# A graph network block: block addresses computed ahead of the adds, and the attention sums' self-loops scaled group by group

## The chip, the cores and the metric

The kernel runs on one core of one Trainium2 chip. The metric is device time of one execution, in microseconds, as the median of several runs. An engine has a queue of its own (its sequencer), which waits for semaphores, loads registers, computes addresses and hands instructions to the engine. PE is TensorE, DVE VectorE, ACT ScalarE, POOL GpSimd, SP SyncE.

## The reference

A graph of 6250 nodes with 256 features and 106,250 edges (each node has an edge to itself, a self-loop, besides 100,000 drawn edges). In order: a normalisation; a graph convolution added to linear attention; a mixture of 8 experts; graph attention with 8 heads of 32 features, added to a second linear attention; and a mixture of 4 experts whose gates come from a second graph attention (131,072 edges, their ends drawn from 8192 numbers, 6250 of which are nodes).

```python
# graph convolution
agg = jax.ops.segment_sum(x[src], dst, num_segments=n)
# graph attention; a loop edge is added to every node
e = a_src[src] + a_dst[dst]
e = jnp.where(e > 0, e, NEG_SLOPE * e)
ex = jnp.exp(e - m[dst])
alpha = ex / (denom[dst] + 1e-16)
out = jax.ops.segment_sum(h[src] * alpha[:, :, None], dst, num_segments=N)
# router: the same attention with 4 heads of 4, then the two best of 4 experts
```

## The kernel before

Nodes are held in 49 blocks (the code calls them windows, W = 49) of 128, one node per partition. Edges are sorted by target block and cut into slots of 128 edges, four slots to a group (GROUP = 4). Four stages walk over groups: the prelude (33 groups, with keys and values of the first linear attention), stage 1 (187 groups, with the 8 experts), stage 2 (220 groups, with keys and values of the second linear attention) and stage 3 (268 groups, with the 4 experts). The order on every engine is written out by hand, and semaphores tie the engines together.

In each group POOL gathers the rows of the edges' source nodes with four indirect DMAs (L365, L1446, L2438, L3086), into a ring of 6, 5, 8 and 10 groups in the four stages. DVE makes a one-hot matrix from the edges' targets, PE multiplies it with the rows (L2468 in stage 2), and DVE adds the four products to the four blocks' sums (L471, L1786, L2659, L3293). Which block a slot belongs to is known only at run time. `windows` loads the four block numbers of a group into registers with one instruction (a TENSOR_LOAD in the trace), and `bass.ds(ws[u], 1)` selects a block; its address is worked out by an instruction of the engine's queue (a FUSED_REGOPS in the trace) in front of the instruction that first uses it. Each add waits for the one before it (s_acc). In stage 2 each also waits for its own product (s_sum); elsewhere one wait per group is enough, since the four products share one count.

In the attention stages (2 and 3) a group takes more steps. PE multiplies the transposed one-hot with the blocks' target scores (`scores`: L2456, L3104), which needs the block numbers too. DVE reduces and adds (`exponents`: L2632, L2636, L2642), ACT takes exponentials, and DVE scales the gathered rows (`message`: L2650). In stage 2 the DVE queue works in this order: load of block numbers, exponents of q + 2, one-hot of q + 5 (L2621), the four adds of q, message of q + 2. For the first 150 groups, one group in three then has the variance of the keys (L2663, L2668, L2669), and the next one the scaling of the values (L2673, L2678); groups 157 to 205 have one add of 128x256 (L2701). POOL's gather of group q + 8 waits for PE's sums of group q.

The self-loops need no gather: R.gat holds each node's own row, [128, 49, 264], 256 features and 8 weights. After the weights' exponential (s_e0) DVE multiplies the features of all 49 blocks by them in one instruction (L2732), ahead of one_hot(4) and of the loop over groups:

```python
v.wait_ge(self.s_e0, 1)
a4 = R.gat[:, :, 0:self.FEAT].rearrange("p t (h c) -> p t h c", h=GH)
st.then(v.tensor_tensor(a4, a4, R.gat[:, :, self.FEAT:GROW].unsqueeze(3).to_broadcast([P, W, GH, GC]), ALU.mult))
one_hot(4)
```

gperm lists the blocks in the order in which groups come to them: a group q has no target outside the first 4q + 4 of the list.

## Time and profile before

| What | us |
|---|---|
| Median of 3 runs | 4643.39 (4642.45 to 4644.51) |
| Span of the profiled execution | 4628.2 |
| What lies around the span, by the median | 15.2 |
| Prelude, first to last add | 229.2 to 400.5 |
| Stage 1, first to last add | 480.0 to 1650.1 |
| Stage 2, first gather, first add, last add's start | 1957.1, 1987.9, 3134.8 |
| Stage 2, end of the last gather of group 2, of group 3 | 1973.0, 1990.9 |
| Stage 3, first gather, last gather, last add's start | 3228.3, 4582.5, 4610.4 |

The profile gives the span of its execution, not its whole time; the last line of the upper part is the median less the span. PE is busy for 82% of the span, DVE for 69%, POOL for 61%, ACT for 49%. These shares are averages over stages that have different limits, so what follows is read stage by stage. "Idle before" a group of instructions is the time in which its engine stood still just ahead of them, and "<-" names what ended it; "issue" means that nothing in the trace was waited for, so that the queue itself was late.

### The profile page before, as it was taken

To read this page: it belongs to the slowest core of one execution; us is meant where nothing else is said; L and a number is where in the kernel's file an instruction comes from. 1 tells how busy PE (TensorE), PEld (TensorE's weight loads), DVE (VectorE), ACT (ScalarE), POOL (GpSimd) and SP (SyncE) were. 2 spreads that over 40 slices of the span, in tenths; PEclk is the share of its full clock that TensorE was granted. 3 is DMA by queue.
4 is the path that set the end of the run, shared out by engine and by line. 5 is a ranking of instruction groups with operands and counts; after the bars stand their busy time and mean duration, and the time that the engine had idled before them with its cause. 6 is when DMAs were issued, how large, how long until landed. Compare 5 with 4: busy or idle time off the path is not lost. (4 is left out here: it accounts for less than half of the span.)

```text
span 4628.2 us, 67760 instructions
## 1 busy us (share of the span) xinstructions
PE 3772.5 (82%) x17777; PEld 2396.7 (52%) x17779; DVE 3181.4 (69%) x10005; ACT 2264.5 (49%) x4090; POOL 2802.1 (61%) x2880
## 2 busy tenths in 40 slices
PE   6797989999989999678888888876187888887876
PEld 6654556666656566444444445445144444444444
DVE  7675566554645554688888888886567777777776
ACT  6342223323232332357767765444366666666665
POOL 0174676665655500177766777773777777777774
PEclk9998999999999999888889988995588889898887
DMA  3333111121211100545555545653322222222221
GB/s 98 77 90 106 39 40 41 32 43 31 43 29 38 26 8 2 160 122 141 141 133 132 132 127 156 163 141 95 56 35 44 40 40 39 39 40 40 39 39 26
DMA packets 291738, 331.33 MB, mean 72 GB/s; under 512 B 80182, under 2 KB 246062, under 8 KB 291366
## 3 DMA queue, kind: packets, MB, share of 16 engines
q0 software_dynamic: 105328, 175.77, 18.5%
q1 hardware_dynamic: 186038, 151.23, 11.8%
q8 instruction: 156, 2.56, 0.2%
q14 instruction: 216, 1.77, 0.1%
HBM read 289.56 MB, written 30.77 MB: 69 GB/s over the span
## 5 line engine op out<-in xcount | busy, mean ns | idle before, releaser
L3086 POOL DMA_INDIRECT st_rows<-tabr,router_rsrc x1072 | 1028.7, 960 | 329.7 <-issue 318.8
L2438 POOL DMA_INDIRECT all_XT<-tab,graph_gsrc x880 | 852.1, 968 | 310.3 <-issue 244.2
L1446 POOL DMA_INDIRECT st_rows<-tab,graph_gsrc x748 | 741.4, 991 | 465.3 <-PE st_pe L1469 262.2
L1699 ACT ACTIVATE st_h<-st_ph,st_shift,st_scale 128x448 f32<-128x448 f32 x448 | 324.0, 723 | 729.6 <-PE st_ph L1557 729.5
L2468 PE MATMUL st_po<-all_XT,st_hot 128*128 128x264 f32 x1760 | 572.5, 462 | 36.6 <-DVE gat_sum L2659 35.3
L2659 DVE TENSOR_TENSOR gat_sum<-gat_sum,st_po 128x264 f32 x880 | 376.0, 427 | 144.8 <-DVE gat_sum L2659 97.9
L3131 PE MATMUL st_px<-all_XT,st_w 128*128 128x512 f32 (+2 forms) x832 | 427.3, 664 | 18.5 <-ACT st_hid L3191 18.5
L2468 PEld LDWEIGHTS st_po<-all_XT,st_hot 128*128 128x128 f32 x1760 | 323.4, 213 | 198.6 <-DVE gat_sum L2659 120.2
L3143 PE MATMUL st_py<-st_w,st_hid 128*128 128x256 f32 x1568 | 424.9, 418 | 0.6 <-ACT st_hid L3191 0.6
L1786 DVE TENSOR_TENSOR gcn_acc<-gcn_acc,st_pe 128x65 f32 x748 | 166.2, 222 | 348.4 <-PE st_pe L1469 257.8
L3104 PE MATMUL st_pad<-st_adr,st_hott 128*128 x1072 | 123.2, 184 | 338.6 <-DVE st_zd L3257 323.6
L1570 PE MATMUL st_po<-all_XT,st_h 128*128 128x256 f32 x1568 | 373.5, 390 | 12.8 <-DVE all_X L1890 9.3
L1557 PE MATMUL st_ph<-st_h,all_XT 128*128 128x448 f32 x896 | 355.3, 547 | 3.3 <-ACT st_h L1699 3.3
L1557 PE MATMUL st_ph<-st_xt,all_XT 128*128 128x448 f32 x896 | 356.9, 552 | 0.0
L1570 PEld LDWEIGHTS st_po<-all_XT,st_h 128*128 128x128 f32 x1568 | 297.9, 195 | 67.5 <-issue 15.1
L3143 PEld LDWEIGHTS st_py<-st_w,st_hid 128*128 128x128 f32 x1568 | 308.0, 207 | 46.1 <-ACT st_hid L3191 1.0
L3104 PEld LDWEIGHTS st_pad<-st_adr,st_hott 128*128 128x128 bf16 x1072 | 87.5, 98 | 446.6 <-issue 425.0
L3293 DVE TENSOR_TENSOR router_racc<-router_racc,st_po 128x60 f32 x1072 | 229.8, 214 | 118.0 <-DVE router_racc L3293 3.2
L3180 ACT ACTIVATE st_rows<-st_d 128x16 f32<-128x16 f32 x268 | 57.9, 216 | 516.9 <-DVE st_d L3267 511.6
L3131 PEld LDWEIGHTS st_px<-all_XT,st_w 128*128 128x128 f32 x832 | 176.1, 223 | 192.0 <-issue 166.5
L1890 DVE SCALAR_TENSOR_TENSOR all_X<-st_po,st_gate,all_X 128x256 f32 x392 | 168.6, 478 | 144.9 <-PE st_po L1570 127.8
L2650 DVE TENSOR_TENSOR all_XT<-all_XT,st_wps 128x1024 f32<-128x1024 f32 x220 | 267.0, 1214 | 0.5 <-ACT all_XT L2575 0.5
(517 smaller groups left out, 7187.1 us busy)
## 6 DMA issues: line engine op xcount, KB each, us to landing
st_bc<-drowr SPq DMA_DIRECT2D x268, 128.0 KB
st_bc<-drow SPq DMA_DIRECT2D x220, 128.0 KB
st_rows<-tabr,router_rsrc POOLq DMA_INDIRECT x1072
all_XT<-tab,graph_gsrc POOLq DMA_INDIRECT x880
st_xtb<-xtd SPq DMA_DIRECT2D x98, 128.0 KB
st_rows<-tab,graph_gsrc POOLq DMA_INDIRECT x748
tab<-gat_sum SPq DMA_DIRECT2D x7, 924.0 KB
xtd<-all_XT SPq DMA_DIRECT2D x49, 128.0 KB, 1.7
```

The costliest lines, as they stand in the source:

```text
L1446: g.indirect_dma_start(self.rows[:, b, u, :], None, self.R.tab0, bass.IndirectOffsetOnAxis(self.R.gsrc[:, t:t + 1], 0)).then_inc(self.s_ro ...
L1557: mm = t.matmul(self.ph[:, m % 3, 0:HALF], (self.w1, self.w2)[l][:, e, i, fb * P:(fb + 1) * P], src[:, i, h * HALF:(h + 1) * HALF], start= ...
L1570: mm = t.matmul(self.po[:, q % 2, j - 2 * k, :], self.h2[:, i, j * P:(j + 1) * P], self.wo[:, e, i, :], start=(i == 0), stop=(i == C - 1))
L1699: a.activation((self.h1, self.h2)[l][:, fb, h * HALF:(h + 1) * HALF], self.ph[:, m % 3, 0:HALF], ACT.Relu, bias=self.shift[:, l, i:i + 1], ...
L2438: g.indirect_dma_start(self.rows[:, b, u, :], None, self.R.tab1, bass.IndirectOffsetOnAxis(self.R.gsrc[:, t:t + 1], 0)).then_inc(self.s_ro ...
L2468: t.matmul(self.po[:, m % self.BANKS, 0:GROW], self.hot[:, q % self.HOTF, u], self.rows[:, q % self.ROWS, u, :], start=True, stop=True).th ...
L2650: v.tensor_tensor(m, m, self.wps[:, :, :].unsqueeze(3).to_broadcast([P, GROUP, GH, GC]), ALU.mult)\
L2659: v.tensor_tensor(aw, aw, self.po[:, (GROUP * q + u) % self.BANKS, 0:GROW], ALU.add).then_inc(self.s_acc, 1)
L3086: g.indirect_dma_start(self.rows[:, b, u, :], None, self.R.tabr, bass.IndirectOffsetOnAxis(self.R.rsrc[:, t:t + 1], 0)).then_inc(self.s_ro ...
L3131: mm = t.matmul(self.px[:, i, 0:n * P], self.w1[:, e, c, fb * P:(fb + 1) * P], R.XT[:, c, r * P:(r + n) * P], start=(c == 0), stop=(c == C ...
L3143: t.matmul(self.py[:, m % 2, 0:D], self.hid[:, (E1 * u + e) % 2, fb, j * P:(j + 1) * P], self.w2[:, e, fb, :], start=(fb == 0), stop=False)
L3293: v.tensor_tensor(aw, aw, self.po[:, q % self.SUMB, u * n:(u + 1) * n], ALU.add).then_inc(self.s_acc, 1)
```

## The change

Four places are touched. `placed` has an engine work out addresses at once. In the prelude, stage 1, stage 2 and stage 3, DVE computes the four blocks' addresses right behind the load of the block numbers, at the group's head; in the prelude and stage 1 that is now ahead of the one-hot as well. PE does the same for `scores` in stages 2 and 3, ahead of its two waits. And in stage 2 the one multiply of the self-loops is gone: in the first 13 groups `own_edges` loads four entries of gperm and multiplies those four blocks, 49 blocks in all, and the adds of these groups wait for s_a0.

```diff
+def placed(engine, aps):
+    for ap in aps:
+        engine.lower_ap(ap)
+    return aps
+
+def columns_of(tile, ws):
+    return [tile[:, bass.ds(w, 1), :].rearrange("p a d -> p (a d)") for w in ws]
...
         def add_edges(q):
+            aws = placed(v, columns_of(acc, self.windows(ENG.DVE, q)))
             one_hot(q + self.HOTS - 1)
-            ws = self.windows(ENG.DVE, q)
             v.wait_ge(self.s_sum, q + 1)
-            for u in range(GROUP):
+            for u, aw in enumerate(aws):
                 if GROUP * q + u:
                     v.wait_ge(self.s_acc, GROUP * q + u)
-                aw = acc[:, bass.ds(ws[u], 1), :].rearrange("p a d -> p (a d)")
                 v.tensor_tensor(aw, aw, self.pe[...], ALU.add).then_inc(self.s_acc, 1)
...
         def scores(q):
-            ws = self.windows(ENG.PE, q)
+            near = placed(t, [self.adl[:, bass.ds(w, 1), :, :].rearrange("p a k h -> p (a k h)")
+                              for w in self.windows(ENG.PE, q)])
             t.wait_ge(self.s_tt, q + 1)
...
+        def own_edges(q):
+            lo, hi = GROUP * q, min(GROUP * q + GROUP, W)
+            if lo >= hi:
+                return
+            _, ws = self.nc.values_load_multi_w_load_instructions(
+                R.gperm[0:1, lo:hi], engines=(ENG.DVE,), min_val=0, max_val=W - 1, ...)
+            for w in ws:
+                a = R.gat[:, bass.ds(w, 1), 0:self.FEAT].rearrange("p a (h c) -> p (a h) c", h=GH)
+                x = R.gat[:, bass.ds(w, 1), self.FEAT:GROW].rearrange("p a h -> p (a h)")
+                v.tensor_tensor(a, a, x.unsqueeze(2).to_broadcast([P, GH, GC]), ALU.mult).then_inc(self.s_a0, 1)
+
+        def add(q, aws):
+            if GROUP * q < W:
+                v.wait_ge(self.s_a0, min(GROUP * q + GROUP, W))
...
         v.wait_ge(self.s_e0, 1)
-        a4 = R.gat[:, :, 0:self.FEAT].rearrange("p t (h c) -> p t h c", h=GH)
-        st.then(v.tensor_tensor(a4, a4, R.gat[:, :, self.FEAT:GROW].unsqueeze(3).to_broadcast([P, W, GH, GC]), ALU.mult))
         one_hot(4)
         for q in range(self.GROUPS):
-            ws = self.windows(ENG.DVE, q)
+            aws = placed(v, columns_of(R.gat, self.windows(ENG.DVE, q)))
+            own_edges(q)
             exponents(q + 2)
             one_hot(q + 5)
-            add(q, ws)
+            add(q, aws)
```

Stage 1's `add_edges` and stage 3's `scores`, `add` and loop get the same edit as the ones shown.

## Rows read from the trace of the kernel before

**Rows 1.** The page: its first line.

```profile
span 4628.2 us, 67760 instructions
```

**Rows 2.** Groups by line: count, busy us, mean ns; then idle before, by releaser.

```profile
L3086 POOL DMA_INDIRECT st_rows<-tabr,router_rsrc x1072 | 1028.7, 960 | 329.7 <-issue 318.8 <-DVE st_part L3284 7.6 <-POOLq L73 3.2
L2438 POOL DMA_INDIRECT all_XT<-tab,graph_gsrc x880 | 852.1, 968 | 310.3 <-issue 244.2 <-PE st_po L2468 65.8 <-POOL st_diag L1010 0.3
...
L2659 DVE TENSOR_TENSOR gat_sum<-gat_sum,st_po 128x264 f32 x880 | 376.0, 427 | 144.8 <-DVE gat_sum L2659 97.9 <-PE st_po L2468 46.8
```

**Rows 3.** Window: length; busy us of PE, PEld, DVE, ACT, POOL; clock, DMA share, GB/s.

```profile
2050.00:2800.00 750.00, 635.69 (x2378) 357.45 (x2376) 631.80 (x1472) 524.42 (x1008) 539.24 (x567) 0.90 0.53 136
```

**Rows 4.** Waits of POOL, 2100 to 2800 us: total us, times, longest.

```profile
POOL all_XT L2438 <- PE st_po L2468: 53.1, 49, 2.5
```

**Rows 5.** Timeline of DVE, one group of stage 2: start, duration, line.

```profile
2499.98 0.36 DVE L2632 TENSOR_REDUCE st_zd<-st_pad 128x64 f32<-128x192 f32 x1 [0.30 <-issue]
2500.38 0.22 DVE L2636 TENSOR_TENSOR st_z<-st_zd,all_XT 128x64 f32<-128x64 f32 x1
...
2501.71 0.43 DVE L2659 TENSOR_TENSOR gat_sum<-gat_sum,st_po 128x264 f32 x1 [0.21 <-DVE gat_sum L2659]
...
2503.34 1.21 DVE L2650 TENSOR_TENSOR all_XT<-all_XT,st_wps 128x1024 f32<-128x1024 f32 x1
...
2504.70 0.69 DVE L2678 TENSOR_TENSOR all_XT<-all_XT,st_rs 128x512 f32<-128x512 f32 x1
2505.31 0.35 DVE L2632 TENSOR_REDUCE st_zd<-st_pad 128x64 f32<-128x192 f32 x1
```

**Rows 6.** Timeline of DVE in stage 3: four adds, next group's first reduction.

```profile
3902.86 1.28 DVE L3293 TENSOR_TENSOR router_racc<-router_racc,st_po 128x60 f32 x4
...
3906.02 0.26 DVE L3257 TENSOR_REDUCE st_zd<-st_pad 128x32 f32<-128x96 f32 x1 [0.23 <-issue]
```

**Rows 7.** Line 3293: its adds, ns least, median, most.

```profile
L3293 DVE TENSOR_TENSOR router_racc<-router_racc,st_po x1072: 201/216/219, 3249.5 to 4610.4; 128x60 f32 x179
```

**Rows 8.** Line 3360: address instructions on DVE's queue (FUSED_REGOPS), and updates.

```profile
L3360 DVEq FUSED_REGOPS  x126: 57/57/57, 3384.1 to 4619.0; - x126
L3360 DVE SCALAR_TENSOR_TENSOR all_X<-all_XT,router_gate,all_X x110: 473/477/485, 3493.0 to 4621.7; 128x256 f32 x110
L3360 DVE SCALAR_TENSOR_TENSOR all_X<-st_py,router_gate,all_X x86: 473/483/486, 3384.2 to 4286.6; 128x256 f32 x86
```

**Rows 9.** Lines 2659 and 2382: address instructions, and loads of block numbers.

```profile
L2659 DVEq FUSED_REGOPS  x880: 57/57/57, 1987.5 to 3134.7; - x176
...
L2382 DVEq TENSOR_LOAD <-graph_gwin x220: 338/342/358, 1986.4 to 3132.3; - x110
```

**Rows 10.** Timeline of DVE, the start of stage 2's loop.

```profile
1973.12 13.22 DVE L2732 TENSOR_TENSOR gat_sum<-gat_sum 128x12544 f32<-128x12544 f32 x1
...
1987.94 0.42 DVE L2659 TENSOR_TENSOR gat_sum<-gat_sum,st_po 128x264 f32 x1
...
1993.39 0.23 DVE L2636 TENSOR_TENSOR st_z<-st_zd,all_XT 128x64 f32<-128x64 f32 x1 [1.71 <-DMA all_XT<-tab,graph_gsrc]
```

**Rows 11.** Timeline of POOL, one gather.

```profile
1973.32 13.83 POOL L2438 DMA_INDIRECT all_XT<-tab,graph_gsrc  x1 [0.30 <-issue]
```

**Rows 12.** Line 491: a multiply of one block's size, both operands in SBUF.

```profile
L491 DVE TENSOR_TENSOR all_XT<-all_XT,pre_rs x49: 424/425/426, 227.6 to 401.2; 128x256 f32<-128x256 f32 x49
```

**Rows 13.** Lines 2438 and 2636: first and last gather and rescoring of stage 2.

```profile
L2438 POOL DMA_INDIRECT all_XT<-tab,graph_gsrc x880: 940/946/13833, 1957.1 to 3118.3; - x176
...
L2636 DVE TENSOR_TENSOR st_z<-st_zd,all_XT x220: 224/225/286, 1968.6 to 3126.5; 128x64 f32<-128x64 f32 x110
```

**Rows 14.** Waits of PE for DVE in the prelude (215 to 420 us).

```profile
PE pre_pacc L399 <- DVE all_XT L495: 12.5, 19, 2.0
```

**Rows 15.** Waits of PE for DVE in stage 1 (480 to 1655 us).

```profile
PE st_side L1510 <- DVE st_xn L1836: 15.7, 10, 2.6
```

**Rows 16.** Waits of DVE in stage 3: for gathered rows.

```profile
DVE st_z L3261 <- DMA st_rows<-tabr,router_rsrc: 92.4, 68, 4.0
```

More of the change, by code:

```diff
@@ L1775, in add_edges @@
             for q in qs:
-                one_hot(q + self.HOTS - 1)
                 t = GROUP * (self.first() + q)
@@ L1780, in add_edges @@
                     skip_runtime_bounds_check_because="a count of at most W - 1 windows")
+                aws = placed(v, columns_of(self.acc, ws))
+                one_hot(q + self.HOTS - 1)
                 v.wait_ge(self.s_sum, q + 1)
-                for u in range(GROUP):
+                for u, aw in enumerate(aws):
                     if GROUP * q + u:
                         v.wait_ge(self.s_acc, GROUP * q + u)
-                    aw = self.acc[:, bass.ds(ws[u], 1), :].rearrange("p a d -> p (a d)")
                     v.tensor_tensor(aw, aw, self.pe[:, q % 2, u * GCOL:(u + 1) * GCOL], ALU.add).then_inc(self.s_acc, 1)
@@ L2455, in scores @@
             for u in range(GROUP):
-                mm = t.matmul(self.pad[:, u].rearrange("p k h -> p (k h)"), self.hott[:, q % self.HOTT, u],
-                              self.adl[:, bass.ds(ws[u], 1), :, :].rearrange("p a k h -> p (a k h)"),
+                mm = t.matmul(self.pad[:, u].rearrange("p k h -> p (k h)"), self.hott[:, q % self.HOTT, u], near[u],
                               start=(u == 0), stop=False, skip_group_check=True)
@@ L2651, in message @@
                 .then_inc(self.s_msg, 1)
-        def add(q, ws):
-            for u in range(GROUP):
+        def own_edges(q):
[3 more added lines that the diff above has]
+            _, ws = self.nc.values_load_multi_w_load_instructions(
+                R.gperm[0:1, lo:hi], engines=(ENG.DVE,), min_val=0, max_val=W - 1,
+                skip_runtime_bounds_check_because="a number of a window")
+            for w in ws:
[5 more added lines that the diff above has]
+                v.wait_ge(self.s_a0, min(GROUP * q + GROUP, W))
+            for u, aw in enumerate(aws):
                 v.wait_ge(self.s_sum, GROUP * q + u + 1)
@@ L2657, in add @@
                     v.wait_ge(self.s_acc, GROUP * q + u)
-                aw = R.gat[:, bass.ds(ws[u], 1), :].rearrange("p a d -> p (a d)")
                 v.tensor_tensor(aw, aw, self.po[:, (GROUP * q + u) % self.BANKS, 0:GROW], ALU.add).then_inc(self.s_acc, 1)
@@ L3096, in scores @@
                 return
-            ws = self.windows(ENG.PE, q)
+            near = placed(t, [self.adr[:, bass.ds(w, 1), :, :].rearrange("p a k h -> p (a k h)")
+                              for w in self.windows(ENG.PE, q)])
             t.wait_ge(self.s_tt, q + 1)
@@ L3103, in scores @@
             for u in range(GROUP):
-                mm = t.matmul(self.pad[:, u].rearrange("p k h -> p (k h)"), self.hott[:, q % self.HOTT, u],
-                              self.adr[:, bass.ds(ws[u], 1), :, :].rearrange("p a k h -> p (a k h)"),
+                mm = t.matmul(self.pad[:, u].rearrange("p k h -> p (k h)"), self.hott[:, q % self.HOTT, u], near[u],
                               start=(u == 0), stop=False, skip_group_check=True)
@@ L3284, in message, with add @@
             v.tensor_tensor(part[:, :, 2, :], rows, part[:, :, 1, :], ALU.subtract).then_inc(self.s_part, 1)
-        def add(q, ws):
+        def add(q, aws):
             v.wait_ge(self.s_sum, q + 1)
             n = PARTS * FROW
-            for u in range(GROUP):
+            for u, aw in enumerate(aws):
                 if GROUP * q + u:
                     v.wait_ge(self.s_acc, GROUP * q + u)
-                aw = R.racc[:, bass.ds(ws[u], 1), :].rearrange("p a d -> p (a d)")
                 v.tensor_tensor(aw, aw, self.po[:, q % self.SUMB, u * n:(u + 1) * n], ALU.add).then_inc(self.s_acc, 1)
@@ L3422, in vector @@
         for q in range(self.GROUPS):
-            ws = self.windows(ENG.DVE, q)
+            aws = placed(v, columns_of(R.racc, self.windows(ENG.DVE, q)))
             exponents(q + 2)
             one_hot(q + 5)
-            add(q, ws)
+            add(q, aws)
             for u in range(len(self.judged)):
```

## Prediction

> **What bounds the kernel now.** I read the page first, then the groups by line, then waits and windows stage by stage, because the share of busy time of the page mixes stages with different limits. The span is 4628.2 us [rows 1] and the median 4643.4, so 15.2 us lie around the span; I make the sum on the span and add these.
>
> Stage 3 is bound by POOL. Its 1072 gathers are busy for 1028.7 us and idle 329.7 between them, of which 318.8 is "issue" (about 0.3 us each) [rows 2]; together that is the 1355 us from its first gather to its last. DVE has room there: it waited 92.4 us for gathered rows, at 68 places [rows 16]. What the change does to DVE in stage 3 should cost nothing while those waits last.
>
> Stage 2 looks the same at first and isn't. A gather takes 0.946 us and 0.3 of issue, so a group takes POOL 5.0 us and 220 groups 1100. From the first gather to the last it took 1161 us [rows 13]. Of the difference one gather alone has 12.9 (13.83 us instead of 0.95 [rows 11]), and POOL waited for PE's sums of eight groups back: 53.1 us in 700 of them, 49 places [rows 4], about 0.3 of each being issue, so some 38; over the whole stage 65.8 us at 78 places [rows 2], so 42. Behind those sums stands DVE: in the 750 us window DVE is busy 632, PE 636 and POOL 539 [rows 3], and in the timeline of a group DVE's instructions follow each other without a hole except in two places: 0.21 us ahead of three of the four adds, and 0.30 ahead of the first reduction [rows 5]. The waits of the adds come to 144.8 us over the stage [rows 2]. So up to about group 150 DVE sets the pace, at some 5.4 us per group (that window holds 138 groups). Behind it DVE has no more keys and values to work on, takes 4.8 us, and lives on the eight groups that POOL is ahead; by the end little of that is left: the last gather ends at 3119.3 (3118.3 and 0.95) and its rows are used at 3126.5 [rows 13].
>
> Stage 1 is PE's, with some waits for DVE (15.7 us at 10 places is the largest [rows 15]). The prelude is nearly PE's, but at 19 places PE waits for DVE's scaling, 12.5 us [rows 14].
>
> **The change, part by part.** First, does an address worked out early stay worked out? Line 3360 says so: 196 updates with only 126 address instructions [rows 8], so an address is used again across waits. I take it that the add then carries no address instruction.
>
> *Adds, the gap ahead of each.* In stage 3 four adds take 1.28 us [rows 6]; one takes 0.216 [rows 7], so the gap is (1.28 - 0.216)/3 - 0.216 = 0.139. Two chained instructions with nothing between them have 0.04 (2500.38 less 2499.98 and 0.36 [rows 5]; 0.034 before rounding). So an address instruction costs 0.105 in a gap, of which 0.057 is its own time [rows 9]. Stage 2 has 0.21, 0.07 more, for its second wait. The first add of a group has no gap, since its address is computed under the one-hot. So DVE gains 3 x 0.105 = 0.32 us per group, 69 over stage 2's 220 groups. Bounds: 0.057 (the duration alone) gives 38; 0.14 gives 92.
>
> *The head.* Four address instructions now stand behind the load of block numbers (0.342 [rows 9]) and ahead of the group's first reduction: 4 x 0.105 = 0.42, between 0.23 (4 x 0.057) and 0.56 (4 x 0.139, as if all of stage 3's gap were the address). Behind the message (1.21 us [rows 5]) this is hidden: the load starts under it, and 0.34 + 0.42 and 0.12 for the queue's own steps is 0.88. Behind the variance (0.17 us) it isn't, and the 0.30 there grows to 0.72: 49 groups. Behind the values' scaling (0.69 us, and the reduction follows with no gap [rows 5]) the load's 0.34 and about 0.13 of overheads use up all but 0.14, so 0.28 shows: 49 groups. Together 49 x 0.42 + 49 x 0.28 = 34 us, all before group 150, where DVE sets the pace. The adds give 48 there.
>
> *The self-loops.* One instruction of 13.22 us goes from in front of the loop [rows 10]. The first add was at 1987.9. It can't move by 13: group 0 also needs the rows of group 2, whose last gather ends at 1973.0, and a gather's rows were used 2.5 us after its end at the soonest (group 3: 1990.9, then 1993.39 [rows 10]); 1975.6 and 0.9 for the rescoring and the one-hot gives 1976.5, 11.4 us earlier, with group 0's four multiplies inside this wait. Two waits of DVE for rows, 3.3 us in all ([rows 10] has the first), are covered by the new work. What comes back: 45 multiplies in groups 1 to 12. Line 491 has the same size, both inputs in SBUF: 0.425 us [rows 12], 0.345 when the next overlaps its end by 0.08, as the reduction at 2505.31 does the scaling ahead of it [rows 5], so 15.5 us. And a second load with its first two addresses, 0.6 us, hidden behind a message, about 0.5 exposed in six groups: 3. Up to group 150 stage 2 comes to -11.4 - 3.3 - 48 + 34 + 15.5 + 3.5 = -9.7.
>
> *The POOL gather that took 13.83 us.* It began 0.2 us after the big multiply and ended 0.8 us after it [rows 10, 11]: DVE's read of two SBUF operands held GpSimd off. With 49 short ones it is held at most 0.35 us at a time, in groups in which DVE is slower than POOL anyway (6.7 us against 5.0 and up to 1.4). I price that at 1.5 us, between 0 and 5.
> The Trainium skill, "SBUF — State Buffer", section "Who interferes with whom", says that a tensor_tensor with both inputs in SBUF takes only the read side of the pair that VectorE shares with GpSimd, and infers that it doesn't stall descriptor generation. The trace here speaks against this inference: 12.9 us. By the page alone the gather would stay long, and the sum would be the second rival below.
>
> *From group 150 on.* No head is exposed, and DVE drops to 4.5 us per group. POOL's 5.0 then decides: it keeps its pace but for the some 3 us of waits behind group 158, and the last rows can be used 2.5 to 3.1 us after their gather instead of 7.2. So -3 - 4.3, and -0.95 for the nine gaps of the last three groups: -8.2, of the 22 that the adds offer.
>
> *The prelude.* Load and addresses (0.34, 0.42 and the queue's steps) move ahead of the one-hot, where only 0.2 us of DVE's work hides them; the adds give back 0.33 and lie no longer behind the load. Per group +0.26 us. Its turns come in threes, two with a group: one has 0.3 to 0.4 us to spare, the other none, and PE waits behind that one. 16 x 0.26 = +4 us (0 to 8).
>
> *Stage 1.* The same edit, but DVE often has 0.7 us of other work in flight, and the gap of 0.17 behind the one-hot goes: -0.3 us per group to nothing. Some 25 waits of PE end a stretch of DVE with three to seven adds. -4 us (-9 to +4).
>
> *PE's scores.* Four address instructions ahead of the wait rather than one ahead of each product. PE waits for st_zd there in most groups, which hides them. Nothing. If that cover were gone: 4 x 0.095 = 0.38 in one group in three, 19 us at most.
>
> *Stage 3.* DVE loses 0.42 at each head (0.23 is exposed there already [rows 6]) and gains 3 x 0.105: +0.1 us per group, under the 92.4 us of waits for rows. The last six groups, behind POOL's last gather, are DVE's: 5 heads +2.1, 6 groups of adds -2.0. Nothing.
>
> Sum: -9.7 - 8.2 + 4 - 4 = -17.9 on the span of 4628.2; with 1.5 for gathers held off by the short multiplies -16.4: 4611.8, and 15.2 around it, 4627.0.
>
> **The rivals.**
> 1. *The head is cheap.* An address instruction without one of the engine's beside it takes 0.057. Then 98 heads cost about 15 instead of 34, and the prelude nothing: 4643.4 - 16.5 - 19 - 3 = about 4605. For it: the duration in [rows 9]. Against: in a gap the same instruction costs 0.105. Chance 0.13.
> 2. *It nearly cancels.* Heads at 0.13 each cost 9 more, multiplies that don't overlap (0.425) 4, and the adds' gap may shrink by less; or the long gather has another cause than the multiply and stays, group 3's rows come at 1993.4 as before, and 11 of the 14.7 us at the start are lost (that alone 0.04): 4638 to 4643. Chance 0.22. This last case is what the page on SBUF, quoted above from the Trainium skill, would have.
> 3. *PE is late.* PE is busy 636 us of 750 [rows 3], as much as DVE. With DVE faster and the addresses ahead of PE's wait, PE sets the pace in the groups with keys and outer products: up to +19, so 4646. Against: in those groups the products are ready over 1 us before their add. Chance 0.08.
> 4. *Slower: the gap stays.* The 0.21 us are the waits' and not the address's; the add pays the same with its address ready, and the heads are paid on top. Then 69 us of gain are gone; before group 150 that is +48, behind it POOL had hidden the rest, and prelude and stage 1 lose about 10 more: 4627 + 48 + 10 = 4685. It decides where the gap stays above 0.17. Against: the gaps of 0.139, 0.21 and 0.04 differ just by what stands in them. Chance 0.07.
>
> The Trainium skill, "VectorE: DVE Perf Modes", section "Rules for kernel authors", asks for fewer DVE instructions rather than fewer semaphores; by it 49 multiplies for one are a loss. The rows give it 49 x 0.345 = 16.9 us against 13.2, a loss of 3.7 in DVE's time, which is in the sum; what stood behind the one multiply isn't in the page's rule.
>
> **How the numbers follow.** The forecast (4612 to 4634) has 0.50. What a measurement of this kernel can tell from no change is about 0.2%, 9.3 us. Faster by more than that (below 4634.1): 0.46 of the forecast and the 0.13 of rival 1, with a little of rival 2, 0.60. Within: 0.27, the most of rival 2, rival 3 and the forecast's edge. Slower: 0.13, rival 4 and the upper ends of 2 and 3. The range takes in rival 1 nearly whole, and rivals 2 and 3, and leaves out rival 4: 4604 to 4648. Without the rivals it would be 4612 to 4640.
>
> **What would show it.** Right: three gaps of 0.10 us instead of 0.21 between the adds of stage 2, and 0.03 instead of 0.14 in stages 1 and 3; 0.72 us ahead of L2632 in 49 groups and about 0.28 in 49 more; no gather of stage 2 over 2 us; the first add at about 1976.5 plus what the prelude and stage 1 shift; POOL still waiting for L2468 between groups 60 and 150; stage 3 as long as before. Wrong: gaps that stay, address instructions still counted once per add besides those of the head, POOL's waits gone before group 150 (then the heads cost less than I think), or PE idle less and DVE waiting for L2468.

## The result and the profile after

Five runs of the changed kernel have a median of 4610.87 us (4605.57 to 4617.77), five of the kernel before 4644.51 (4642.45 to 4647.89): the ratio is 0.9928, with a 95% interval of 0.9916 to 0.9940, 33.6 us less. The forecast was 4627.0, 16.4 less. It named the right side and its range (4604 to 4648) held the time, but the gain is twice as large, and a good part of it isn't made where the forecast put it. The profiled execution took 4611.07 us with a span of 4609.3.

The page of the changed kernel, its span and the three groups that answer to [rows 1, 2] (count, busy us, mean ns; idle before):

```profile
span 4609.3 us, 65451 instructions
...
L3110 POOL DMA_INDIRECT st_rows<-tabr,router_rsrc x1072 | 1037.2, 968 | 329.8 <-issue 319.4
L2449 POOL DMA_INDIRECT all_XT<-tab,graph_gsrc x880 | 845.7, 961 | 292.0 <-issue 249.6
...
L2684 DVE TENSOR_TENSOR gat_sum<-gat_sum,st_po 128x264 f32 x880 | 375.9, 427 | 71.6 <-PE st_po L2479 2.7
```

The adds of stage 2 cost the same 427 ns, with 71.6 us of idle time ahead of them instead of 144.8. There are 2309 instructions less: 2832 address instructions at the adds and 1952 at the score products are gone, and half as many have come at the heads (1416 and 976); `own_edges` adds 110 (48 multiplies, 49 address instructions, 13 loads), and 27 semaphore instructions are gone. Stage 2's gathers hold 6 us less and wait 18 us less. Stage 3's gathers are 8.5 us longer in sum, which the forecast didn't have.

The window of [rows 3] and the wait of [rows 4] in the changed kernel:

```profile
2050.00:2800.00 750.00, 594.52 (x2473) 362.12 (x2470) 660.13 (x1528) 536.88 (x1036) 550.86 (x577) 0.91 0.54 139
```

```profile
POOL all_XT L2449 <- PE st_po L2479: 34.9, 37, 2.3
```

DVE is busy for 660 us of 750 rather than 632: it has less idle time, not less work. PE's busy time fell from 636 to 595, so it is now the one with room. POOL waits 34.9 us for the sums in this stretch instead of 53.1, and still waits: DVE still sets the pace, though by less.

DVE's timeline over one group and the start of the next, as in [rows 5]:

```profile
2485.45 0.17 DVE L2694 TENSOR_TENSOR st_var<-st_ssum 128x8 f32<-128x8 f32 x1
2486.18 0.36 DVE L2643 TENSOR_REDUCE st_zd<-st_pad 128x64 f32<-128x192 f32 x1 [0.56 <-issue]
...
2487.27 2.02 DVE L2684 TENSOR_TENSOR gat_sum<-gat_sum,st_po 128x264 f32 x4
2489.21 1.22 DVE L2661 TENSOR_TENSOR all_XT<-all_XT,st_wps 128x1024 f32<-128x1024 f32 x1
...
2490.57 0.69 DVE L2703 TENSOR_TENSOR all_XT<-all_XT,st_rs 128x512 f32<-128x512 f32 x1
2491.30 0.36 DVE L2643 TENSOR_REDUCE st_zd<-st_pad 128x64 f32<-128x192 f32 x1
```

Four adds stand in 2.02 us, so each gap is (2.02 - 4 x 0.427)/3 = 0.104 us. Ahead of the first reduction there are 0.56 us behind the variance, and 0.04 behind the values' scaling (2491.30 less 2491.26). The forecast had 0.72 and 0.28. The rows of line 112, the helper `placed`, say why (least, median, most ns):

```profile
L112 DVEq FUSED_REGOPS  x1416: 93/93/105, 231.1 to 4590.6; - x177
L112 PEldq FUSED_REGOPS  x976: 74/74/78, 1957.3 to 4573.0; - x196
```

The 33, 187, 220 and 268 groups of the four stages have 708 heads, and 1416 instructions are two for each: **one instruction computes two addresses** (so have the 49 multiplies of `own_edges`, with two addresses each, 49 such instructions of 93 ns). It takes 0.093 us instead of 0.057, and two of them, with 0.124 from one start to the next, add 0.25 us to a head.

The first gathers under the short multiplies, in POOL's timeline (against [rows 11]), and the first and last of stage 2 (against [rows 13]):

```profile
1974.05 1.10 POOL L2449 DMA_INDIRECT all_XT<-tab,graph_gsrc  x1 [0.30 <-issue]
1975.46 1.04 POOL L2449 DMA_INDIRECT all_XT<-tab,graph_gsrc  x1 [0.31 <-issue]
```

```profile
L2449 POOL DMA_INDIRECT all_XT<-tab,graph_gsrc x880: 940/946/1694, 1957.9 to 3094.3; - x176
L2684 DVE TENSOR_TENSOR gat_sum<-gat_sum,st_po x880: 414/429/433, 1976.7 to 3106.2; 128x264 f32 x176
```

**Stage lengths.** The four stages are separated by other work, so each can be measured by itself. The table gives, from the rows of each line's first and last instruction, the end of the prelude's last add; from there to the end of stage 1's last add; and from first gather to last add's end in stages 2 and 3. The last column counts stage 3's gathers of over 1.05 us. All rows ran on chips on which the kernel before takes 4642 to 4651 us.

```
                                prelude  stage 1  stage 2  stage 3  long gathers
before, first trace              400.8   1249.6   1178.1   1382.3      32
before, again (e0)               403.2   1259.6   1178.3   1379.2      24
self-loops only (e1)             400.9   1259.4   1181.2   1384.9      30
stage 2's adds only (e3)         402.3   1261.1   1145.4   1386.2      37
stage 1 and scores only (e9)     402.5   1244.8   1176.8   1384.4      37
change, first trace              403.5   1244.9   1148.8   1392.1      84
change, again (e8)               404.0   1245.0   1148.1   1391.2      94
change without self-loops (e2)   403.6   1244.6   1141.9   1390.4      76
early heads (e10)                403.0   1244.6   1121.6   1385.4      37
early heads, one multiply (e11)  402.8   1245.3   1129.7   1383.3      41
```

Two traces of one kernel differ by at most 0.7 us in stage 2, 3.1 in stage 3 and 2.4 in the prelude; the seven traces without stage 3's edit spread over 7 us there. In stage 1 the first trace of the kernel before is 10 us shorter than three others without the edit: that trace was a quick draw, and most of what the forecast took for "15.2 us around the span" is this.

### The profile page after: what moved, and what is told of

It is laid out like the page before. It is cut to its first block and busy times, and to the rows that moved or that the text cites. A ratio compares the mean times of both kernels' runs of the same rounds, so it can differ in the third digit from the quotient of the medians.

```text
span 4609.3 us, 65451 instructions
## 1 busy us (share of the span) xinstructions
PE 3643.4 (79%) x17777; PEld 2357.9 (51%) x17779; DVE 3191.2 (69%) x10053; ACT 2265.3 (49%) x4090; POOL 2793.7 (61%) x2880
## 5 line engine op out<-in xcount | busy, mean ns | idle before, releaser
L1457 POOL DMA_INDIRECT st_rows<-tab,graph_gsrc x748 | 730.3, 976 | 470.7 <-PE st_pe L1480 269.5
L2479 PE MATMUL st_po<-all_XT,st_hot 128*128 128x264 f32 x1760 | 528.5, 451 | 81.5 <-DVE gat_sum L2684 79.7
L2479 PEld LDWEIGHTS st_po<-all_XT,st_hot 128*128 128x128 f32 x1760 | 342.9, 215 | 183.1 <-issue 86.3
L2684 DVE TENSOR_TENSOR gat_sum<-gat_sum,st_po 128x264 f32 x880 | 375.9, 427 | 71.6 <-PE st_po L2479 2.7
L3129 PE MATMUL st_pad<-st_adr,st_hott 128*128 x1072 | 68.2, 176 | 399.7 <-DVE st_zd L3281 386.6
L3129 PEld LDWEIGHTS st_pad<-st_adr,st_hott 128*128 128x128 bf16 x1072 | 51.2, 98 | 490.4 <-issue 410.8
L1568 PEld LDWEIGHTS st_ph<-st_h,all_XT 128*128 128x128 f32 x896 | 172.4, 196 | 152.2 <-issue 127.8
```

What stands on the lines that cost most here:

```text
L1457: g.indirect_dma_start(self.rows[:, b, u, :], None, self.R.tab0, bass.IndirectOffsetOnAxis(self.R.gsrc[:, t:t + 1], 0)).then_inc(self.s_ro ...
L1568: mm = t.matmul(self.ph[:, m % 3, 0:HALF], (self.w1, self.w2)[l][:, e, i, fb * P:(fb + 1) * P], src[:, i, h * HALF:(h + 1) * HALF], start= ...
L2479: t.matmul(self.po[:, m % self.BANKS, 0:GROW], self.hot[:, q % self.HOTF, u], self.rows[:, q % self.ROWS, u, :], start=True, stop=True).th ...
L2684: v.tensor_tensor(aw, aw, self.po[:, (GROUP * q + u) % self.BANKS, 0:GROW], ALU.add).then_inc(self.s_acc, 1)
```

## The experiments

Twelve runs follow; e0 and e8 repeat the kernel before and the changed one. Each ratio is against runs of the kernel before on the same chip, with its 95% interval.

**e0, the kernel before once more**, with no edit.

> The kernel before, unchanged, profiled once more. Between the two traces stage 3 grew by 9.8 us (first gather to last add) where the forecast had nothing, and the mean of its 1072 gathers went from 0.960 to 0.968 us, which is 8.6 us. Theory A: this is the spread between executions, the first trace of the kernel before was a quick one (span 4628.2 against a median of 4643 to 4644): here the span is 4635 to 4648 and the stage 3 gathers have a mean of 0.965 us or more. Theory B: the change made the gathers of stage 3 slower: here they have 0.960 again and the span is about 4628. Time: 4644.5 within 5 us by both.

Measured: 4649.21 us, ratio 1.0003 (0.9995 to 1.0012); the profiled execution took 4644.26. Page and stage 3's gathers and adds:

```profile
span 4642.6 us, 67760 instructions
```

```profile
L3086 POOL DMA_INDIRECT st_rows<-tabr,router_rsrc x1072: 940/944/3785, 3245.7 to 4597.3; - x179
L3293 DVE TENSOR_TENSOR router_racc<-router_racc,st_po x1072: 201/216/219, 3267.3 to 4624.8; 128x60 f32 x179
```

Each theory got one half. The span is 4642.6 as theory A had it, and only 1.7 us lie around it. But the gathers of stage 3 have a mean of 0.957 us (1026.1 in sum), as theory B had it: what was quick in the first trace was mainly stage 1 (10 us of 14.4), and stage 3's lengthening is the change's.

**e1, the self-loops alone.** The adds as before; the multiplies in 13 groups.

```diff
-        st.then(v.tensor_tensor(a4, a4, R.gat[:, :, self.FEAT:GROW]..., ALU.mult))
...
             ws = self.windows(ENG.DVE, q)
+            own_edges(q)
             exponents(q + 2)
```

> The kernel before with the self-loops scaled in the first 13 groups, the addresses left at the adds. Theory A (VectorE sets the pace of stage 2 up to group 150): first add 11.4 earlier and waits for rows 3.3 fewer, against 45 multiplies of 0.335 us (15.1) and some 4 for loads and addresses: +4 at group 150 and nearly that at the end, 4645 to 4651. Theory B (the long POOL gather is what costs, and with it gone the stage ends earlier): about 13 us less, 4631. Both expect no gather of stage 2 over 2 us.

Measured: 4653.8 against 4650.77 us, ratio 1.0010 (1.0001 to 1.0019). Its gathers of stage 2 (least, median, most ns):

```profile
L2438 POOL DMA_INDIRECT all_XT<-tab,graph_gsrc x880: 941/949/1712, 1967.7 to 3132.5; - x176
```

The longest gather is 1.71 us instead of 13.84, and nothing is won: the stage is 3 us longer. Theory B falls. While DVE sets the pace, POOL's 12.9 us only turn into waits; its idle time there grew from 310 to 321 us. The page on SBUF in the Trainium skill ("SBUF — State Buffer", section "Who interferes with whom") infers that a tensor_tensor doesn't stall descriptor generation; these gathers speak against that inference, and the measurement decides. The same section of the Trainium skill also has a rule that the forecast passed over, that a VectorE instruction with two SBUF inputs contends with a GpSimd instruction that reads SBUF. The gather reads its row numbers from SBUF (`gsrc`), so by that rule it would be held, and here the trace agrees (13.83 us).

**e2, addresses alone**: the changed kernel with the one multiply back ahead of the loop.

```diff
+        st.then(v.tensor_tensor(a4, a4, R.gat[:, :, self.FEAT:GROW]..., ALU.mult))
         one_hot(4)
...
-            own_edges(q)
```

> The changed kernel with the self-loops scaled in the one multiply ahead of the loop again. Theory A (a head costs 0.25 us where exposed, as two addresses go in one instruction of 0.093 us at a pitch of 0.124): up to group 150 the adds give 48 us and the heads take 17, so 31; with +2.7 in the prelude and -4.6 in stage 1 the time is 4609 to 4616, the same as with the whole change or up to 4 us less. Theory B (the forecast's head of 0.42 us): 48 less 34 up to group 150, 8 behind it, about 4622. Theory C (the long POOL gather counts): 10 to 13 us slower than the changed kernel, about 4622 too, but then with the VectorE gaps of theory A in the trace.

Measured: 4602.85 against 4650.77 us, ratio 0.9907 (0.9895 to 0.9920). So without the self-loops' part the change is faster: 1141.9 us in stage 2 against 1148.8 and 1148.1. Theory A has the side but not the size: its range began some 8 us too high (4609 against 0.9907 x 4644.5 = 4601). Its sum took stage 1 from the quick trace, and the self-loops' part turned out worth 7 us, not up to 4. Theories B and C fall.

**e3, the adds of stage 2 alone**: `placed` and `columns_of` at the head of stage 2's groups, all else as before.

```diff
-            ws = self.windows(ENG.DVE, q)
+            aws = placed(v, columns_of(R.gat, self.windows(ENG.DVE, q)))
             exponents(q + 2)
```

> The kernel before with the addresses at the head in stage 2's adds alone. Theory A: all the gain is made here, 4610 to 4617, within 4 us of the kernel with the addresses at the head everywhere (prelude +2.7, stage 1 -4.6). Theory B (the forecast's prices): 4644.5 - 14 - 8 = about 4622. If the scores, stage 1 or stage 3 hold a part of the gain that the stages of the trace don't show, this is 5 us or more slower than the run with addresses alone.

Measured: 4616.13 against 4650.77 us, ratio 0.9931 (0.9918 to 0.9944). This one edit has as large a gain as the whole change. Stage 2 went from 1178.3 to 1145.4, 33 us, where the forecast's prices had 22 (48 - 34 up to group 150, 8 behind it). Theory A's time is met, but not its second half: this kernel is 13.3 us slower than e2 on the same chip, not within 4. So the parts outside stage 2 hold a gain too, and the table has it in stage 1 (1261.1 against 1244.6 us), with stage 3 taking 4 us back.

**e4 to e7 ran on another chip**, on which the kernel before takes 5494.5 us. The same product there, and in e8 on a chip of the first kind (busy us, mean ns):

```profile
L3169 PE MATMUL st_py<-st_w,st_hid 128*128 128x256 f32 x1568 | 516.1, 486 | 7.8 <-issue 6.9 <-ACT st_hid L3217 0.9
```

```profile
L3167 PE MATMUL st_py<-st_w,st_hid 128*128 128x256 f32 x1568 | 418.7, 413 | 0.9 <-ACT st_hid L3215 0.9
```

The mean granted clock is 0.857 in the first (e6) and 0.900 in the second. But a slower TensorE is the smaller part of it: the median of that product is 379 ns in both, PE is busy for 3858.8 us in e6 and 3643.4 in the changed kernel, 215 more where the span is 793 longer, and in e6's stage 3 PE is busy for only 1059 us of 1830. There PE waits 563 us for DVE's reduction and POOL 455 us for DVE's operands (POOL is idle for 754 us instead of 330), and three large waits of DVE, put down to DMA transfers, stand there that the changed kernel on the first kind of chip doesn't have (3555 to 5385 us; total us, times, longest):

```profile
DVE router_racc L3318 <- DMA all_XT<-in_m_wout: 138.2, 31, 7.5
DVE all_XT L3398 <- DMA st_brow<-in_m_bout: 129.9, 35, 6.7
...
DVE all_X L3385 <- DMA st_brow<-in_m_bout: 120.5, 35, 6.3
```

So something that DVE waits for comes late. What it is, and why on this chip, stays open, since many of the DMA's completion events are missing from this chip's traces. The lower clock (0.78 in e6's stage 3, 0.85 in the changed kernel's) goes with a TensorE that stands still more; which of the two causes the other isn't shown. These times are therefore no test of the prices, and only what the rows show is used.

**e4, 49 multiplies ahead of the loop.**

```diff
+        for k in range(W):
+            a4 = R.gat[:, k, 0:self.FEAT].rearrange("p (h c) -> p h c", h=GH)
+            v.tensor_tensor(a4, a4, R.gat[:, k, self.FEAT:GROW]..., ALU.mult)
         one_hot(4)
```

> The changed kernel with the self-loops scaled in 49 multiplies of one node block each, all ahead of the loop (addresses fixed in the code), nothing of them in the groups. Theory A (VectorE sets the pace up to group 150, and a gather is held only while the one multiply in flight lasts): no gather of stage 2 over 2 us, the first add 3.2 us later than with the one multiply (49 x 0.335 for 13.2), and stage 2 from first gather to last add 1143 to 1147 us, against 1141.9 with the one multiply and 1148.8 with the change. Theory B (the long gather's 12.9 us set the stage's end): 1130 to 1135. Theory C (VectorE holds GpSimd off over the whole chain of multiplies): a gather of some 15 us is still there.

Measured on that chip: 5422.08 us, ratio 0.9862 (0.9836 to 0.9888).

```profile
L2449 POOL DMA_INDIRECT all_XT<-tab,graph_gsrc x880: 940/946/1687, 2142.7 to 3441.2; - x176
```

Theory C falls: the same work in 49 pieces, back to back, holds no gather over 1.69 us. A gather is held only until the multiply in flight ends. Between A and B this run doesn't tell; e11 does.

**e5, each head twice.** A second load and a second set of addresses, by which the adds write.

```diff
             aws = placed(v, columns_of(R.gat, self.windows(ENG.DVE, q)))
+            outs = placed(v, columns_of(R.gat, self.windows(ENG.DVE, q)))
```

> The changed kernel with each head of stage 2 twice: the block numbers loaded and the four addresses worked out a second time, and the adds write by the second set. One more head is 0.38 for the load and 0.25 for two address instructions. Theory A: 0.63 us in the 92 groups in which it follows the variance or the values' scaling, 58 us up to group 150, nothing behind a message, of which the 16 us that VectorE waits for rows at the end give back some: stage 2 is 36 to 50 us longer than the 1148.8 of the change. Theory B (an address instruction costs 0.105 each, four in a head): 0.80 x 92 = 74, 52 to 66 longer. Theory C (heads are hidden anyway): under 10 longer.

Measured on that chip: 5419.2 us, ratio 0.9861 (0.9836 to 0.9886). DVE's timeline, the reduction behind a variance:

```profile
2514.39 0.17 DVE L2694 TENSOR_TENSOR st_var<-st_ssum 128x8 f32<-128x8 f32 x1
2515.75 0.36 DVE L2643 TENSOR_REDUCE st_zd<-st_pad 128x64 f32<-128x192 f32 x1 [1.19 <-issue]
```

The gap is 1.19 us against 0.56 with one head: 0.63, the price of 0.38 for the load and 0.25 for four addresses, and not theory B's 0.80. Its effect on the end (stage 2 is 13 us longer than in e6) can't be read on a chip where DVE waits for other things, so theory C isn't settled by it.

**e6, the next head behind this message**, on the changed kernel.

```diff
         for q in range(self.GROUPS):
-            aws = placed(v, columns_of(R.gat, self.windows(ENG.DVE, q)))
...
             message(q + 2)
+            if q + 1 < self.GROUPS:
+                aws = placed(v, columns_of(R.gat, self.windows(ENG.DVE, q + 1)))
```

> The changed kernel with the head of stage 2's next group issued right behind the message of this one, ahead of the variance and the values' scaling, so that load and addresses lie under the 1.21 us of the message. Theory A: the gap ahead of the first reduction goes from 0.554 to 0.035 us behind the variance and from 0.03 to -0.08 behind the scaling, 29 us up to group 150; PoolE's gathers (845.7 us and 268.5 between them) then end the stage: 1126 to 1131 us from first gather to last add against 1148.8, the time 18 to 22 us less than with the change, 0.988 of before. Theory B (TensorE is close behind VectorE and becomes the bound): half of that or less.

Measured on that chip: 5412.3 us, ratio 0.9846 (0.9825 to 0.9867), the lowest of the four, though its interval overlaps those of e4 and e5. The reduction behind a variance now starts 0.08 us before that instruction's recorded end, where it came 0.55 behind it, so the head is hidden; what that is worth can't be read here. e10 has the same edit on the first kind of chip.

**e7, scores and stage 3's adds alone**, on the kernel before.

> The kernel before with two parts of the change: TensorE's score products with their four addresses ahead of the wait (stages 2 and 3), and stage 3's adds with addresses at the head. Theory A (the edit of stage 3 shifts VectorE's comparison so that it is more often in flight 0.13 us into a gather, and holds it): stage 3 from first gather to last add 1388 to 1394 us against 1379 to 1386 in four kernels without it, 70 to 100 gathers over 1.05 us against 32; stage 2 unchanged or 3 us less by the scores; in all 4 to 9 us slower than before. Theory B (the forecast: nothing from either): within 3 us of before, stage 3 below 1387.

Measured on that chip: 5446.25 us, ratio 0.9905 (0.9882 to 0.9927). Both theories are wrong there: on this chip these two parts give 48 us. By which of the two, and in which stage, stays open, since no trace of the kernel before was taken on that chip, nor was the change itself run there. What they do on the first kind of chip, e9 and e10 show.

**e8, the changed kernel again**, beside the next three.

> The changed kernel once more, beside the next three on the same chip. On the chip of the first two sets: 0.9928 of before within 0.0015. Stage lengths on such a chip: last add of the prelude to last add of stage 1 1244 to 1247 us (1244.9), stage 2 from first gather to last add 1147 to 1151 (1148.8), stage 3 from first gather to last add 1388 to 1394 (1392.1). Theory A (the trace's stages repeat within some 3 us): all three so. Theory B (stage 3's 8 us more were the spread of single executions): stage 3 in 1379 to 1386 here. On a chip like the one of the third set (before at 5494) the ratio is near 0.986 and the lengths say nothing.

Measured: 4608.45 against 4642.5 us, ratio 0.9924 (0.9911 to 0.9937). Theory A: 1245.0, 1148.1 and 1391.2 us.

**e9, stage 1 and the scores alone**, on the kernel before.

```diff
             for q in qs:
-                one_hot(q + self.HOTS - 1)
                 t = GROUP * (self.first() + q)
                 _, ws = ...
+                aws = placed(v, columns_of(self.acc, ws))
+                one_hot(q + self.HOTS - 1)
```

> The kernel before with two parts of the change whose effects lie in different stages: stage 1's head (load, addresses, then comparison), and TensorE's score products with their addresses ahead of the wait in stages 2 and 3; adds of stages 2 and 3 and the self-loops as before. Theory A (read from the stages of the runs so far): stage 1 takes 1243 to 1247 us against 1259 to 1261, stage 2 1173 to 1178 against 1178.2, stage 3 1379 to 1386: 0.9960 of before within 0.0015. Theory B (the forecast: 4 us from stage 1, nothing from the scores): 0.999. Theory C (the scores are what lengthened stage 3): stage 3 1388 or more.

Measured: 4630.16 against 4642.5 us, ratio 0.9969 (0.9957 to 0.9980). Theory A in all: 1244.8 in stage 1, 1176.8 in stage 2 (1.4 less by the scores), 1384.4 in stage 3. So the scores don't lengthen stage 3, and its adds' edit is left; e10 takes that one out of the changed kernel.

**e10, early heads**: e6's edit, and stage 3's adds as before the change.

> The changed kernel with stage 2's next head behind this group's message, and stage 3's adds as before the change. Theory A: stage 2 ends with the gathers, 1126 to 1131 us against 1148.8; stage 3 1379 to 1386 with about 32 gathers over 1.05 us against 86: 25 to 30 us less than with the change, 0.987 of before. Theory B (TensorE comes next at once): stage 2 1138 to 1145, 0.990. Theory C (the edit of stage 3's adds has nothing to do with its length): stage 3 1388 to 1394.

Measured: 4571.2 against 4642.5 us, ratio 0.9842 (0.9830 to 0.9855). Its gathers of stage 2, and a reduction behind a values' scaling:

```profile
L2449 POOL DMA_INDIRECT all_XT<-tab,graph_gsrc x880 | 842.8, 958 | 268.3 <-issue 258.8
```

```profile
2482.05 0.69 DVE L2703 TENSOR_TENSOR all_XT<-all_XT,st_rs 128x512 f32<-128x512 f32 x1
2482.66 0.35 DVE L2643 TENSOR_REDUCE st_zd<-st_pad 128x64 f32<-128x192 f32 x1
```

POOL's waits for PE over the stage (total us, times, longest):

```profile
POOL all_XT L2449 <- PE st_po L2479: 9.1, 30, 0.3
```

The gap is gone (2482.66 lies 0.08 before the end of the scaling), and so are POOL's waits: 268.3 us for 880 gathers is 0.305 each, the issue time alone, and the longest put down to PE is 0.3, which is that same issue time. Now POOL alone sets the length: 842.8 + 268 + 10.8 behind its last gather is 1121.6 us. Theory A has the mechanism, its floor for stage 2 was 4 us too high, and the time is 37 us below e8's where it had 25 to 30 (31.4 between the two spans: 26.5 in stage 2, 5.8 in stage 3). B falls. Stage 3 is back at 1385.4 with 37 long gathers: theory C falls.

**e11, the same with the one multiply.**

> The kernel above with the self-loops in the one multiply ahead of the loop, so that one gather is held for 13.8 us. Theory A (with the heads hidden PoolE's gathers set the end of stage 2, so the long gather now costs): stage 2 1134 to 1140 us, 6 to 12 us slower than with the self-loops in the groups. Theory B (VectorE still sets the pace, the 49 multiplies cost their 19 us): 5 to 8 us faster than it, as in the pair without early heads (1141.9 against 1148.8).

Measured: 4580.65 against 4642.5 us, ratio 0.9863 (0.9848 to 0.9878). POOL's timeline:

```profile
1970.16 0.95 POOL L2449 DMA_INDIRECT all_XT<-tab,graph_gsrc  x1 [0.30 <-issue]
1971.41 13.92 POOL L2449 DMA_INDIRECT all_XT<-tab,graph_gsrc  x1 [0.30 <-issue]
```

Theory A in the difference: stage 2 is 8.1 us longer than in e10 and the time 9.5 (6 to 12 expected), while the length of 1129.7 lies 4 us under its range, by the same floor. The gathers are busy for 8.5 us more (851.3 against 842.8). Scaling the self-loops in the groups, which costs 7 us in the pair of the change and e2, gives 8 here. The sign is set by which engine is the bound.

## Why the prediction was half of it

Step by step, with the lengths of the table. What the forecast had is told first.

- **Adds, the gap**: 0.105 us less each, 48 up to group 150. Measured: 0.211 to 0.104 in stage 2, and up to group 150 the gaps ahead of the second to fourth adds fell from 97.6 to 49.0 us, 48.6 less. Right. Rival 4 (the gap stays) is refuted by the same rows, rival 3 (PE late) by PE's 595 us and by e10, in which the stage ends with POOL.
- **The head**: four address instructions of 0.105 each, 0.42 us, 34 us in 98 groups. Here is **the step that failed**. The trace has two instructions of 0.093 us for four addresses, 0.25 us. Up to group 150 the time ahead of L2643 behind variance and scaling grew by 11.0 and 5.6 us, 16.6 instead of 34 (in 92 groups; in six more the multiplies of `own_edges` stand ahead of the reduction, and e2, which has none there, shows 18.3 in all 98). Rival 1, at 0.057 for an address, had nearly this price (0.25/4 = 0.062) for another reason, and got 0.13 of the chances. That its 4605 lies nearer to the measured time than 4627 is in part luck: it had 35 us for stage 2, where 29 were measured, and nothing more for stage 1. The kernel before has address instructions of 57 ns only [rows 8, 9], one address each, so its trace couldn't show that four computed in a row come as two; the lower bound in the forecast, 0.23, did cover it.
- **The self-loops**: +4.3 us up to group 150 in all (-11.4 - 3.3 + 15.5 + 3.5). Measured: the first add comes 18.8 us behind the first gather instead of 30.8, 12.0 earlier; e1 comes to group 150 4.0 us later than e0 (851.5 against 847.5), and its stage 2 is 3 us longer. Right. The multiplies follow at 0.335 us. The pair of the change and e2 has +7, 5.6 of it up to group 150.
- **The long gather** gone, with little gain before POOL is the bound: right, by e1. The "nearly cancels" rival is refuted where it lets the gather stay.
- **From group 150 on**: -8.2 and 1.5 for held gathers. From the stage's start to group 150's first add DVE gained 24.7 us (847.5 to 822.8), over the whole stage 29.3, so 4.6 fell behind it. Right in kind. The last gather now ends 11.4 us before the last add does, instead of 16.0.
- **The prelude**: +4. Means of five and five preludes without and with the edit: 401.9 and 403.4, +1.5, hardly clear of the spread. As a head costs 0.17 us less than priced, 16 x (0.26 - 0.17) = 1.4 is what the forecast's own sum then gives.
- **Stage 1**: -4, from -9 to +4. Measured: 1244.6 to 1245.3 in six traces with the edit; 1259.4 to 1261.1 in three without, 1249.6 in the fourth. So -15 against three and -5 against one. Two parts can be told apart. Ahead of stage 1's first add there are 79 us in the first trace, e1 and e9, 86 in e0 and e3, and 81 to 82 in the changed kernels, so this part goes its own way without any edit. In the first 200 us the granted clock differs too: 0.80 in e0, 0.84 in the changed kernel.

```profile
400.00:600.00 200.00, 161.67 (x723) 103.31 (x724) 101.92 (x310) 44.59 (x65) 99.30 (x102) 0.80 0.27 72
```

```profile
400.00:600.00 200.00, 161.99 (x742) 102.71 (x740) 105.79 (x318) 47.23 (x69) 103.13 (x107) 0.84 0.27 73
```

  The first line is e0's, the second the changed kernel's (columns as in [rows 3]). The first trace of before has 0.87 there and e1 0.86. From the first add to the last it takes 1170.1, 1173.2, 1174.6 and 1180.3 us without the edit and 1162.7 to 1165.7 with it, and PE's waits for DVE in this stretch add up to 54.5 to 57.2 us without and 46.7 to 47.4 with it. So the edit gives some 9 us (8 to 10) through these waits. The rest of the difference is PE's busy time, 1086.5 to 1096.3 us in the four traces without any edit of stage 1, and the stretch ahead of the first add. The runs' times agree: e9 is 9 to 20 us faster than before, and 1.4 of it lie in stage 2. The forecast had the mechanism (waits of PE for DVE) and too little of it, -4 for -9; its heads were priced at 0.42 here as well.
- **PE's scores**: nothing. 1.4 us in stage 2 (e9). Right on this chip.
- **Stage 3**: nothing, as DVE has room. Measured: +7.5 (means of 1391.2 in three traces with the adds' edit, 1383.7 in seven without). The step was wrong in a way that no price would mend: DVE's extra 0.25 us don't cost DVE anything, they move its one-hot. In the traces without the edit, 11 to 24 of the 268 one-hots start more than 1.1 us behind a gather's start; with it, 49 to 60. A gather starts 1.25 us after the last, so these run on into the next one. How far they run is what counts: where the one-hot ended within 0.15 us of a gather's start, or began after it, the gather took 0.94 to 0.95 us in the mean, as usual; one that ran on for 0.25 to 0.30 us went with gathers of 1.09, and 0.35 to 0.40 with 1.18. In the first trace of before 57 one-hots ended within 0.05 us of a gather's start; in the changed kernel 3 did, and 39 ended 0.25 to 0.30 us behind it, a shift by the 0.25 us of a head. Gathers of over 1.05 us under no one-hot are 12 to 18 in every one of the ten traces. The changed kernel shows one, DVE above and POOL below:

```profile
3375.22 0.42 DVE L3270 TENSOR_TENSOR st_hotb<-st_count,router_rdrel 128x512 bf16<-128x512 bf16 x1
```

```profile
3374.05 0.94 POOL L3110 DMA_INDIRECT st_rows<-tabr,router_rsrc  x1 [0.30 <-issue]
3375.30 1.16 POOL L3110 DMA_INDIRECT st_rows<-tabr,router_rsrc  x1 [0.30 <-issue]
```

  The one-hot runs until 3375.64, and the gather that began under it takes 0.22 us more than its neighbour. The forecast knew that a DVE operation with two SBUF operands holds a gather, priced it in stage 2 and didn't ask it of stage 3, where POOL is the bound and every held gather counts in full.
- **The 15.2 us around the span**: wrong, and harmless. It is 1.7, and the other 13 were the quick trace; with 1.7 around it that execution took 4630, and none of the 52 timed ones of the kernel before on chips of this kind took under 4637.1. Why it was so quick stays open. As the forecast added its sum to the median, nothing came of it; the sum of -16.4 stands as it was made.

By terms: the forecast's -16.4, with -12.9 for stage 2 (16 less for heads, 3 back), -10.6 for stage 1 (measured against the usual 1259.6, so with some 5 us that aren't the edit's), -2.5 for the prelude and +7.5 for stage 3, is -34.9; measured were -33.6. That the range held is owed in part to stage 3, whose unforeseen 7.5 us took back a part of what the other stages gained beyond the forecast: without them the time would have been about 4603.4, just below the range.

The best version is e10: 4571.2 us, 71 less than before and 37 less than the change, on one chip. Its stage 2 is bound by POOL, and what is left there is the 0.305 us between gathers.

## What to carry to other kernels

Register work costs only where it stands behind a short operation: load and compute the next iteration's addresses right behind the longest operation of this one, and it is free. Where an engine can hold the bound engine's work, as DVE held POOL's gathers here, its idle time says nothing of the cost of giving it more; ask what will be in flight when the bound engine's next transfer begins. And profile the kernel before twice before taking the difference of span and median for an overhead: here one draw was 14 us off.

## What the hardware showed beyond that

- Four addresses computed together are two instructions of 93 ns on DVE's queue and two of 74 ns on PE's; one address computed alone was 57 and 46 ns.
- An operation of DVE that reads two SBUF operands and is still in flight some 0.13 us into a gather of GpSimd lengthens that gather by what it has left to run then: the multiply of 13.22 us ended 13.02 us into the gather, which took 13.83 (0.94 and 12.89). Under the same work in 49 pieces back to back no gather took over 1.69 us. A one-hot of 0.42 us that ended 0.34 us into a gather made it 1.16. No run here tests an operation with one operand in SBUF.
- Two chips ran the same kernel in 4644 and 5494 us. On the slower one the mean of a TensorE product was 486 ns instead of 413 while its median was 379 on both, and two parts of the change (e7) were worth 48 us of which the first kind of chip shows nothing.
